# Score products over all 128 rows of the array, in both attentions of a transformer layer on one core

## The reference, cut to what matters

```python
# first attention, causal, for each batch b and head h
se    = (q @ k.T) / 4                                      # Euclidean scores
inner = -q_hyp[:, :1] @ k_hyp[:, :1].T + q_hyp[:, 1:] @ k_hyp[:, 1:].T
dist  = arccosh(max(-inner, 1 + 1e-6))
s     = (1 - alpha) * se + alpha * (-dist**2 / curv_k)     # alpha: one number for each row and head
y     = softmax(where(causal, s, -inf)) * spike_mask @ v
x     = layernorm(x + y @ Wout.T + bout)
# second attention, not causal, then 8 experts of which each token takes 2
h     = layernorm(x) * g + b
x     = x + softmax(q(h) @ k(h).T / 4) @ v(h) @ Wo
out   = layernorm(x + x + moe(layernorm(x)))
```

## Time and profile before

| what | us |
|---|---|
| runs | 2506.71, 2522.12, 2525.76; median 2522.12 |
| span of the profiled execution | 2506.3 |
| first attention, first to last constant or score product | 97 to 1137 |
| second attention, first sP to last values | 1201 to 1912 |
| experts and end | 1945 to 2506 |
| busy over the span: PE, DVE, ACT, POOL | 2144.7, 1616.9, 1493.8, 595.6 |
| mean granted TensorE clock | 0.855 |

### The profile page before, as it was taken

One profiled execution on the slowest core, in us unless ns is written; L12 is line 12 of the kernel. 1 busy time (PEld: TensorE's weight loads), 2 busy tenths in 40 slices (PEclk: granted clock), 3 DMA queues, 4 the chain that ended last, 5 costly groups with the idle time before them and its releaser, 6 DMA issues. The chain is left out here.

```text
span 2506.3 us, 39194 instructions
## 1 busy us (share of the span) xinstructions
PE 2144.7 (86%) x12525; PEld 1129.4 (45%) x12526; DVE 1616.9 (65%) x3495; ACT 1493.8 (60%) x2762; POOL 595.6 (24%) x636
## 2 busy tenths in 40 slices
PE   4799998999998999996788988888886399999990
PEld 2344454444454544443222232222223288888880
DVE  4477777877777887774566656566661655555556
ACT  1387888878797978993256565565664143333332
POOL 4330404131323232112111112111012123333320
PEclk9678898979798989897789887777777599999995
DMA  1220212111111211101402232452532811111116
GB/s 43 62 70 21 64 39 59 43 55 47 51 51 40 56 37 54 41 12 43 59 25 37 43 60 92 111 144 87 142 119 76 349 38 48 44 47 45 46 38 210
DMA packets 140068, 172.38 MB, mean 69 GB/s; under 512 B 23873, under 2 KB 120338, under 8 KB 137874
## 3 DMA queue, kind: packets, MB, share of 16 engines
q1 hardware_dynamic: 131426, 149.58, 21.3%
q0 software_dynamic: 7488, 20.46, 2.7%
q10 hardware_dynamic: 1008, 0.54, 0.1%
HBM read 105.47 MB, written 65.01 MB: 68 GB/s over the span
## 5 line engine op out<-in xcount | busy, mean ns | idle before, releaser
L1273 DVE TENSOR_REDUCE NM<-sP 128x1 f32<-128x512 f32 x512 | 332.4, 684 | 231.0 <-PE sP L1152 229.2
L1083 ACT ACTIVATE PT<-tP 128x512 f32<-128x512 f32 x512 | 285.8, 603 | 262.8 <-PE tP L1164 261.2
L703 DVE CUSTOM_DVE_ANT_0 YZ<-SeP,YZ 128x512 f32<-128x512 f32 (+3 forms) x512 | 243.8, 487 | 189.8 <-PE SeP L563 166.9
L477 ACT ACTIVATE YZ<-YZ,gsc 128x512 f32<-128x512 f32 (+3 forms) x512 | 327.1, 667 | 57.8 <-DVE YZ L692 57.6
L1519 ACT ACTIVATE H<-hP,B1T 128x256 f32<-128x256 f32 x312 | 126.9, 472 | 271.5 <-PE hP L1598 206.9
L455 ACT ACTIVATE XL<-mP 128x512 f32<-128x512 f32 (+1 forms) x384 | 206.3, 537 | 68.9 <-PE mP L573 67.4
L588 PE MATMUL tPa<-ident,YZ 128*128 128x128 f32 x1280 | 245.4, 310 | 1.2 <-ACT PTa L463 0.8
L463 ACT ACTIVATE PTa<-tPa 128x512 f32<-128x512 f32 (+1 forms) x384 | 208.8, 544 | 41.0 <-PE tPa L594 36.0
L1152 PE MATMUL sP<-STGb 48*128 48x512 f16 x512 | 171.4, 448 | 42.7 <-DVE NM L1273 35.7
L692 DVE SCALAR_TENSOR_TENSOR YZ<-YZ,XL 128x1280 f32<-128x1280 f32 x128 | 195.7, 1529 | 18.6 <-ACT YZ L469 17.7
L562 PE MATMUL SeP<-STG 48*128 48x512 f16 (+3 forms) x512 | 168.9, 330 | 45.1 <-DVE mn L703 44.4
(11 more groups left out here) (303 smaller groups left out, 4153.0 us busy)
## 6 DMA issues: line engine op xcount, KB each, us to landing
STG<-planes_a_scratch SPq DMA_DIRECT2D x512, 32.0 KB, 1.9
X<-in_L_ffn_W SPq DMA_DIRECT2D x32, 512.0 KB, 4.2
weight_planes<-X SPq DMA_DIRECT2D x64, 256.0 KB, 2.3
STGb<-planes_scratch SPq DMA_DIRECT2D x96, 128.0 KB, 7.0
planes_a_scratch<-HI SPq DMA_DIRECT2D x64, 128.0 KB, 1.7
planes_a_scratch<-LO SPq DMA_DIRECT2D x64, 128.0 KB, 1.8
STG<-planes_a_scratch SPq DMA_DIRECT2D x128, 64.0 KB, 2.1
Y<-results_scratch SPq DMA_DIRECT2D x16, 512.0 KB, 8.8
```

The source lines that it names most:

```text
L477: act.activation(w, w, ACT.Square, bias=gsc[:, b % 2, 1, i, hh:hh + 1], scale=gsc[:, b % 2, 0, i, hh:hh + 1]).then_inc(hyp_ready, 1)
L703: dve.tensor_tensor_reduce(out=w, in0=SeP[tc % 2][:, 0:W[i]], in1=w, scale=1.0, scalar=3e38, op0=ALU.add, op1=ALU.min, accum_out=mn[:, h % ...
L1083: act.activation(PT[:, p % 4, par, kt, :], tP[x % 3][:, :], ACT.Exp).then_inc(exp_done, 1)
L1273: dve.tensor_reduce(NM[:, g % 2, col:col + 1], sP[n % 2][:, :], AX.X, ALU.max, negate=True).then_inc(max_done, 1)
```

## The change

In the first attention the staging tile is replaced by two. SMV holds the moving side (keys) of a pair of heads, the even head in rows 0 to 47, the odd one in 64 to 111, 4 pairs deep. SST holds the stationary side (queries) twice, once for each head of the pair, with zeros in the rows of the other head. So a product takes all 128 rows and the zero rows add nothing. Loads go by pairs of heads (12 transfers of 32 KB) in place of groups of four heads (20 transfers of 32 and 64 KB). The constant products and `columns` are taken out.

In the second attention STK holds the keys of both heads and STQ the queries with zeros in the other head's rows; sP contracts over 112 rows, tP over 114. The ring has three half batches in place of two batches, a half being 12 transfers of 64 KB, and the first half is loaded at slot step -3 in place of -5. The values' tile is packed to 17 columns a head; the product still takes 32 columns of it, and the columns that belong to the next head come out in rows that nobody reads. The zeros and constants are written by POOL (STQ) and DVE (STK).

```diff
-            STGS = 3
+            STGS = 4
+            LOADS = 16 * 2 * 6
...
-            KEEP = 1700
...
-            STG = sb(ctx, "STG", [P, STGS, 4, 2, T], F16)
+            SST = sb(ctx, "SST", [P, STGS, 2, 2, T], F16)
+            SMV = sb(ctx, "SMV", [P, STGS, 2, T], F16)
...
+                    pool.memset(SST[:, :, :, :, :].rearrange("p g o r t -> p (g o r t)").bitcast(F32), 0.0).then_inc(setup_pool, 1)
+                    pool.memset(SMV[:, :, 0, :], 0.0).then_inc(setup_pool, 1)
+                    pool.memset(SMV[:, :, 1, :], -LOG_OFFSET).then_inc(setup_pool, 1)
+                    pool.wait_ge(setup_pool, 8)
                     for par in range(2):
-                        pool.memset(STG[64 * par + 32:64 * par + 64, :, 2, :, :], 1.0).then_inc(setup_pool, 1)
-                        pool.wait_ge(setup_pool, 6 + 2 * par)
-                        pool.memset(STG[64 * par + 32:64 * par + 64, :, 3, :, :], -LOG_OFFSET).then_inc(setup_pool, 1)
-                        pool.wait_ge(setup_pool, 7 + 2 * par)
+                        pool.memset(SST[64 * par + 32:64 * par + 64, :, 1, par, :], 1.0 / 16).then_inc(setup_pool, 1)
...
-                        g = at_group(n, -16)
-                        if g is not None:
-                            b, gg = g // NG, g % NG
-                            if gg == 0:
+                        pr = at_pair(n, -12)
...
-                            if g >= STGS:
-                                sp.wait_ge(se_full, G * NT * (g - STGS + 1))
-                            rows = planes_d[b % 2].rearrange("l (o c) (q s r d) t -> l c q s r d o t", c=CH, q=2, s=2, r=2)
-                            for s in range(2):
-                                for par in range(2):
-                                    dst = 64 * par
-                                    hi, lo = rows[0, gg // 2, gg % 2, s, par], rows[1, gg // 2, gg % 2, s, par]
-                                    sp.dma_start(STG[dst:dst + D, g % STGS, :, s, :], hi).then_inc(staged[g % STGS], 16)
-                                    for qk in range(2):
-                                        first, second = (hi, lo) if qk == 0 else (lo, hi)
-                                        sp.dma_start(STG[dst + D:dst + 2 * D, g % STGS, qk:4:2, s, :],
-                                                     first[:, qk:4:2]).then_inc(staged[g % STGS], 16)
-                                        sp.dma_start(STG[dst + 2 * D:dst + 3 * D, g % STGS, qk:4:2, s, :],
-                                                     second[:, qk:4:2]).then_inc(staged[g % STGS], 16)
+                            if pr >= STGS:
+                                sp.wait_ge(se_full, 2 * NT * (pr - STGS + 1))
+                            rows = planes_d[b % 2].rearrange("l (o c) (s r d) t -> l c s r d o t", c=CH, s=NG, r=2)
+                            for par in range(2):
+                                hi, lo = rows[0, pp // NG, pp % NG, par], rows[1, pp // NG, pp % NG, par]
+                                for jj, (still, moving) in enumerate([(hi, hi), (hi, lo), (lo, hi)]):
+                                    dst = 64 * par + D * jj
+                                    sp.dma_start(SST[dst:dst + D, pr % STGS, :, par, :], still[:, 0:4:2]).then_inc(staged[pr % STGS], 16)
+                                    sp.dma_start(SMV[dst:dst + D, pr % STGS, :, :], moving[:, 1:4:2]).then_inc(staged[pr % STGS], 16)
...
                     def op(h, o, lo, hi):
-                        j = h % G
-                        depth = R3 + 1 if o >= 2 else R3
-                        return STG[64 * (j % 2):64 * (j % 2) + depth, (h // G) % STGS, o, j // 2, lo:hi]
+                        if o % 2 == 0:
+                            return SST[:, (h // 2) % STGS, o // 2, h % 2, lo:hi]
+                        return SMV[:, (h // 2) % STGS, o // 2, lo:hi]
...
-                        if 0 <= s < HEADS - 1:
-                            spare = 3 * s + min(t + 1, 3)
-                            for f in range((KEEP - columns(n)) // T):
-                                if f == 0 and spare >= 2:
-                                    pe.wait_ge(ln_ready, spare - 1)
-                                pe.matmul(mP[spare % 2][:, :], identb[:, :], identb[:, :].unsqueeze(1).broadcast_to([P, NT, P]),
-                                          start=True, stop=True)
...
+            STQ = sb(ctx, "STQ", [P, RING, 2, HALF, T], F16)
+            STK = sb(ctx, "STK", [P, RING, HALF, T], F16)
+            VS = sb(ctx, "VS", [P, 2, NT * H * (D + 1) + 16])
+            VV = VS[:, :, 0:NT * H * (D + 1)].rearrange("p s (r d) -> p s r d", d=D + 1)
...
-                        for half in range(2):
-                            b = at_batch(n, -5, 2 + 8 * half)
-                            if b is None or b >= 2:
-                                b = at_batch(n, -3, 3 + 2 * half)
-                                b = None if b is None or b < 2 else b
-                            if b is not None:
-                                if half == 0:
-                                    if b == 0:
-                                        sp.wait_ge(stg_set, 2)
-                                    sp.wait_ge(pl_stored, 32 * b + 32)
-                                    if b >= 2:
-                                        sp.wait_ge(t_full, NP * TP * (b - 1))
-                                par = half
+                        k = at_half(n, -3, 1)
+                        if k is not None:
+                            b = k // 2
+                            if k == 0:
+                                sp.wait_ge(stg_set, 4)
+                            sp.wait_ge(pl_stored, 32 * b + 32)
+                            if k >= RING:
+                                sp.wait_ge(t_full, HALF * TP * (k - RING + 1))
+                            for par in range(2):
                                 for jj, planes in [(0, (0, 0)), (1, (0, 1)), (2, (1, 0))]:
-                                    for qk in range(2):
-                                        src = planes_d[b % 2, planes[qk], 2 * qk:2 * qk + 2].rearrange("c (hh r d) t -> r d (c hh) t", r=2, d=D)
-                                        dst = 64 * par + D * jj
-                                        sp.dma_start(STG[dst:dst + D, b % 2, qk, :, :], src[par]).then_inc(staged[b % 2], 16)
+                                    dst = 64 * par + D * jj
+                                    q, key = [planes_d[b % 2, planes[qk], CH * qk + k % 2].rearrange("(hh r d) t -> r d hh t", r=2, d=D)[par]
+                                              for qk in range(2)]
+                                    sp.dma_start(STQ[dst:dst + D, k % RING, par, :, :], q).then_inc(staged[k % RING], 16)
+                                    sp.dma_start(STK[dst:dst + D, k % RING, :, :], key).then_inc(staged[k % RING], 16)
...
+                            if b == 0:
+                                pool.memset(STQ[:, :, :, :, :].rearrange("p g r q t -> p (g r q t)").bitcast(F32), 0.0).then_inc(stg_set, 1)
...
-                            base = 64 * par
-                            pe.matmul(sP[n % 2][:, :], STG[base:base + R3, b % 2, 0, q, i * P:(i + 1) * P],
-                                      STG[base:base + R3, b % 2, 1, q, :], start=True, stop=True).then_inc(s_full, 1)
+                            pe.matmul(sP[n % 2][:, :], STQ[0:DEPTH, k % RING, par, q, i * P:(i + 1) * P],
+                                      STK[0:DEPTH, k % RING, q, :], start=True, stop=True).then_inc(s_full, 1)
...
+                            pe.matmul(tP[x % 3][:, :], STK[0:AUG, k % RING, q, kt * P:(kt + 1) * P],
+                                      STQ[0:AUG, k % RING, par, q, :], start=True, stop=True).then_inc(t_full, 1)
...
-                                mm = pe.matmul(avP[32 * j:32 * (j + 1), :], VS[:, b % 2, kt, G * (g % NG) + j, :],
+                                col = (H * kt + G * (g % NG) + j) * (D + 1)
+                                mm = pe.matmul(avP[32 * j:32 * (j + 1), :], VS[:, b % 2, col:col + 32],
...
-                                dve.memset(STG[64 * par + 32:64 * par + 64, :, 1, :, :], SHIFT).then_inc(stg_set, 1)
+                            dve.memset(STK[0:64, :, :, :].rearrange("p g q t -> p (g q t)").bitcast(F32), 0.0).then_inc(stg_set, 1)
+                            dve.memset(STK[64:96, :, :, :].rearrange("p g q t -> p (g q t)").bitcast(F32), 0.0).then_inc(stg_set, 1)
+                            dve.memset(STK[96:128, :, :, :], SHIFT).then_inc(stg_set, 1)
...
```

More of the change, by code:

```diff
@@ L218, in _ @@
                 def _(pe):
-                    pe.wait_ge(setup_pool, 14)
+                    pe.wait_ge(setup_pool, 15)
                     pe.wait_ge(a_w_loaded, 64)
@@ L325, in at_group, with at_pair @@
                 return d // (SUB * G) if d % (SUB * G) == 0 and 0 <= d // (SUB * G) < GROUPS else None
+            def at_pair(n, offset):
+                d = n - offset
```

(18 more changed lines are left out.)

59 lines of the change are left out of this document (18 added, 41 removed).

## The result

| | before | changed |
|---|---|---|
| median, us | 2514.6 (2506.71 to 2525.76, 4 runs) | 2352.22 (2349.44 to 2354.95, 4 runs) |
| span of the profiled execution, us | 2506.3 | 2353.2 |
| mean granted clock | 0.855 | 0.904 |

The ratio is 0.9363, 95% interval 0.9324 to 0.9402: 6.4% faster. The forecast was 2385, 33 us above what was measured.

What follows compares the result with a forecast made beforehand. PE was taken to bound both attentions. From 2506.3 us, first attention -75, second attention -44 and loads -6 gave a span of 2381; 4 added for the runs' median made 2385, range 2310 to 2485.

Steps and rivals of the forecast that it cites:

- Passages of the first attention: First attention: each change between product shapes costs PE 0.10 to 0.11 us; full rows save 20 us a batch.
- The bound of the first attention: First attention: ACT replaces PE as bound, with DVE holding the batch head; 120.2 us a batch, 68 us less for six.
- The first batch: First attention, first batch: saves as much as the last batch, 3.5 us.
- Constant products: First attention: removing them saves 2 of their 4.5 us a batch; they also keep PE active for the clock.
- rival 3: Both attentions: empty rows don't count for the clock and constant products are missed; clock 0.65, 2700 us; chance 0.06.
- The clock: Second attention: score products of 112 and 114 rows keep the clock better, raising it from 0.79 to 0.895.
- The overlap: Second attention: about 305 of 512 possible pairs of products no longer run side by side, 64 us more for PE.
- The passages: Second attention: 46 changes between product shapes a batch, 0.1 us each, give 37 us back.
- Loads: First attention's loads by pairs cost nothing; half the bytes first at the second attention's start saves 6 us.
- Rival 1: ACT and DVE run denser, second attention's clock nearly 1: -113 and -80 for the two attentions, 2310 us; chance 0.12.
- Rival 2: Both attentions: the clock follows PE's busy time, not rows; first saves 37, second loses 34, 2497 us; chance 0.11.
- Rival 4: First attention: loads by pairs come late, PE starts 64 pairs 2 us late, 128 us, 2510 us; chance 0.05.

Runs made afterwards that it cites:

- e6: Changed kernel, but the first attention's score products take only each head's own 64 rows: 2446.43 us, ratio 0.9715 to the kernel before.
- e1: Kernel before with only the first attention's part of the change, the second attention left as before: 2397.77 us, ratio 0.9568.
- e4: Changed kernel with the constant products put back at the same places: 2359.14 us, ratio 0.9409 to the kernel before.
- e11: Changed kernel, but both score products of the second attention take each head's own 64 rows, with overlap and passages back: 2384.03 us.
- e2: Kernel before with only the second attention's part of the change, the first attention and its constant products left as before: 2469.57 us, ratio 0.9814.
- e3: Kernel before with only its constant products taken out: 2509.81 us, ratio 0.9986.
- e8: Changed kernel, but sP and tP of the second attention contract over rows 0 to 71, without overlap: 2411.59 us.
- e7: Changed kernel, but in the second attention sP takes rows 0 to 47 and tP 0 to 49 for both heads, without overlap: 2492.4 us.
- e5: Changed kernel, but both operands of the first attention's score products are cut to rows 0 to 71: 2361.19 us, ratio 0.9387 to the kernel before.

## Why the prediction was right, and where its sizes were off

**Passages of the first attention.** Right in kind and size. The prediction took 20 us of PE time a batch; e6 has 20.3. PE at "about 98 us" a batch came out at 97.39 in the fourth and at some 94 in the others.

**The bound of the first attention.** ACT and the batch's head under DVE, 120.2 us a batch: 119.0 to 119.5 were measured in five of the six and 116.7 in the sixth. The head's 20.50 us window still has DVE at 19.47.

**The first batch.** This term was mis-sized: 3.5 us taken, 18.4 measured. I set it equal to the last batch without a window of it. One would have shown the difference, before:

```profile
124.30:245.20 120.90, 115.08 (x587) 55.04 (x586) 87.94 (x205) 98.87 (x176) 28.13 (x26) 0.81 0.17 49
```

ACT is busy for 82% of it, in the last batch for 92%; PE was busy for 115.08 at a clock of 0.81. By the prediction's own rule, 98.87/0.95 = 104.1, it had 16.8 to give. This is 15 of the 28 us between the forecast span (2381) and the measured one.

**The start.** The 7.8 us there are no gain of the change that could be shown. The first DG comes at 116.5 to 122.5 in the profiles with the changed first attention (changed kernel, e1, e4 to e11) and at 117.5 to 124.3 in those with the old one (before, e2, e3): the two overlap.

**Six batches.** 76.2 for 68: about 1 us a batch in five, where 119.2 stand for 120.2, and 3.5 in the sixth.

**Constant products.** Counted at 2 us a batch; e3's full batches are 1.9 shorter than those of the kernel before and 3.6 shorter than e2's. They also held the clock up, which rival 3 used: most clearly in the last batch (e3), and without any gain of time once the rows are 128 (e4).

**The second attention.** -44 forecast, -37.7 measured. Three of its terms were off, and the sum came out better than its parts.

*The clock.* 0.895 taken, 0.92 measured. e8 shows that the clock goes with the rows, taken or filled, as was said. But the row that the prediction leant on most doesn't show it: in the stretch from 183.8 on, at 0.50 with PE busy throughout, PE issues the same score products, transposes and products with the values as in the stretch at 1.00 just before (149.7 to 183.8). What came between is a wait of PE for DVE:

```profile
183.51 0.28 PE L562 MATMUL SeP<-STG 48*128 48x256 f16 x1 [1.37 <-DVE mn L703]
```

*The overlap.* 64 us of PE's work taken, some 54 by e7. In the trace of the kernel before, 118 pairs of sP and 117 of tP start within 0.1 us of each other. These are 235 of 512 possible pairs, not 305, and at 0.21 us each they make 49 us. The prediction took all covered time for whole pairs; part of it belongs to products that start more than 0.1 us apart.

*The passages.* 37 us taken back, from 46 passages a batch. The trace of the kernel before has 241 in the whole stage (30 a batch) between a score product and a full-shape one without a wait in between, at some 0.09 us each: 22 us. e8 against e7 makes it 20. The passages to the values' products stayed: from tP to these it takes 0.31 us before (1333.42 to 1333.73) and after (1190.37 to 1190.68).

PE's full-rate work was to rise by 27 us. By the two counts it rose by 49 - 22 = 27, by busy time and clock from 493 (616.09 x 0.80) to 535, by 42; the second estimate differs by 4 even between e8 and the changed kernel, with the same products. Either way both terms were too large by about 15, and that they cancelled was luck.

By the rule of the Trainium skill ("TensorE: Matmul & The Clock Gate", Part 3, Packing small matmuls) that the prediction set beside its own sum, all 512 pairs run together and the loss is 108 us of work; the trace has under half of them, and 49 to 54.

**Loads.** -6 forecast, -7.0 measured; no wait for a staging tile shows within the batches.

**The rivals.** Rival 1 (2310) came nearer for the first attention alone: 100.4 us there, nearer to its 113 than to my 75. In the second attention it had -80, and 37.7 came. Rival 2 (busy time sets the clock) falls by e8. Rival 3 (zero rows don't count, the constant products are missed) falls by the clock of 0.92 in both attentions, where it needed less than 0.83, and by e4; that zero rows count at all rests on e11 against e1. Rival 4 (late loads) falls by the 119 us batches.

**Still open.** How much of the second attention's clock comes from rows of zeros and how much from rows of data isn't settled, as said above. Nor is it why 72 rows did nearly as well as 128 in the first attention (922.8 and 913.2 us) and not in the second. In the first attention PE has room: a batch of e5 takes 119.0 us, with PE busy for 94.89 of them and ACT for 106.00, so that a lower clock there costs little. That is an argument, not a test.

## What to carry to other kernels

Look at PE's timeline for products of another shape of array than their neighbours': where the spacing of 512 columns is 0.32 us in place of 0.21, filling up with zero rows may pay (they cost PE no time here, 0.21 us for 512 columns with 128 rows), and the engine behind PE in busy time says how much of it comes out. Where two small products already run side by side, count in the timeline how many pairs start together before giving it up: the overlap was worth 93 us here (e7 against e1), and only the better clock of full rows and the fewer passages together paid for it. And cut a window for the first and the last batch each, since what is true of one needn't be of the other.

## What the runs showed of the hardware

- The granted clock rose with the rows of the score products at equal columns: second attention 0.80 with 72 rows, 0.92 with 112 and 114, 0.93 with 112 and 128, at a lower busy share of PE. (With 72 rows most data of the odd heads is missing as well.) It rose from 0.81 to 0.84 where nearly all of the added rows held zeros in one operand (e1 and e11).
- Products of an identity with itself, which nobody reads, held the clock up: without them it was 0.835 to 0.845 in ten executions, with them 0.843 to 0.863 in thirteen (e3).
- After a product of 48, 49 or 64 rows the weights of a full-shape product are loaded only 0.32 us after its start (PEld idle for 0.23 us in between), and likewise those of a product of few rows after a full-shape one (0.16 us for a mask product of 128 columns, in place of 0.06). Between products of 72 or more rows the load goes under the product before (0.21). The Trainium skill ("TensorE: Matmul & The Clock Gate", Part 3, The mechanism) lists that a weight load overlaps with running products only when the row group differs, though a line above it also allows a load into a background buffer. The trace disagrees with the first and fits the second: between two products of the same 128 rows the load of 0.10 us is hidden.
- 72 rows behave as the full shape in this respect, 64 don't (e5 and e6: 922.8 and 1006.8 us for the stage).
